# Gathers of a graph network issued in pairs, each pair behind a point of VectorE's work

## The chip, the cores and the metric

One core of a Trainium2 chip runs the whole program, in one launch. The metric is the device time of the launch in microseconds, the median of several runs; lower is better.

## What is computed

A graph of 3125 nodes and 100000 edges, sorted by destination. `x` (3125 x 64) goes through a graph transformer of four layers (hidden width 128, 8 heads of 16), is added to the input and normed, then goes through one message-passing layer, and is again added and normed. Cut to what matters here:

```python
h = gelu(x @ Wi.T + bi)
for i in range(4):                                   # the four layers
    q = (h @ Wq[i].T + bq[i])[dst]                   # per edge, 8 heads x 16
    k = (h @ Wk[i].T + bk[i])[src]                   # gathered per edge
    v = (h @ Wv[i].T + bv[i])[src]                   # gathered per edge
    alpha = sum(q * k, -1) / 4
    a = softmax of alpha over the edges with one dst
    out = segment_sum(a * v, dst)
    x_r = h @ Ws[i].T + bs[i]
    beta = sigmoid([out, x_r, out - x_r] @ Wbeta[i].T)
    h = layer_norm(beta * x_r + (1 - beta) * out + h)
    h = gelu(h @ W1[i].T + b1[i]) @ W2[i].T + b2[i] + h
x = layernorm(x + h @ Wo.T + bo)
msg = silu([x[src], x[dst], rbf(length)] @ mw1 + mb1) @ mw2 + mb2
agg = segment_sum(msg, dst) / count
out = layer_norm(silu([x, agg] @ uw1 + ub1) @ uw2 + ub2)
x = layernorm(x + out)
```

## The kernel before

**Places and chunks.** Nodes are held in 25 blocks of 128 (NB). The edges are cut into 806 places (PLACES) of 128 edges, so that the edges that a place counts have their destinations in one block. 16 places (CH) are a chunk; a pass over all edges has 51 chunks (CHUNKS), the last with 6 places. There are five passes: one for each of the four transformer layers and one for the messages. A chunk's places are handled in four groups of four (G, NG).

**The gather.** For each place GpSimd issues one indirect DMA (L508), which fetches 128 rows of a table in HBM into `slots`, one row a partition: 264 floats of keys and values from `kv_table` in a layer, 128 floats from `src_table` in the message pass. `slots` is a ring of four chunks (RING): chunk c lies in ring position c mod 4. The row numbers of a chunk (`idx`) are loaded by SyncE into the same ring.

**What a layer does with a chunk.** The functions called `attend_step` stand once for each engine, in the same order of chunks. While the step of chunk g is at work, chunk g + 1 is prepared:

- TensorE spreads the queries to the edges with turned one-hots (`spread_terms` L797, `rows` L806); VectorE multiplies them with the fetched keys (`multiply`, L1282, semaphore `spread_used`; it waits for the landing of the group's fetches, `kv_in`, and for the spread queries, `q_spread`) and sums over each head (`sum_heads`, L1288).
- VectorE scans for the running maxima, ScalarE takes exponentials; VectorE weighs the fetched values by them (`weigh`, L1361, `w_done`).
- TensorE multiplies the weighed values of each place with its one-hots (`add_up`, L825). The last matmul of a group frees the group's slots (`slot_free[k][j]`).
- VectorE adds the 16 products to `acc` (`add_place`, L1265, `acc_done` goes up by one a place).

In the message pass `messages` (L1416) takes the place of `multiply`, and there are no scans.

**A layer's head and end.** At the end of a layer VectorE, ScalarE and TensorE norm and feed forward in five groups of blocks. The next layer's keys and values are evicted to `kvst` (L1458) and stored by SyncE to `kv_table`; when all five stores have landed (`tab_out`) the next layer's fetches may go. `begin_layer` on VectorE then evicts the 25 blocks of queries (L1464, `q_ev` goes up by one a block), clears `acc` (L1467, `acc_zero`), makes the first one-hots, weighs 25 blocks (L1476), and multiplies the four groups of chunk 0. `acc` holds the activations that TensorE reads for the queries until then.

**What orders the fetches.** GpSimd's program holds nothing but the fetches until the end (`gather_chunk`). Fetches of a group of a chunk wait for the table, for the chunk's `idx`, and for `slot_free` of the same group four chunks before. So GpSimd may be up to four chunks ahead of VectorE's additions, and goes in fours:

```python
for j in range(groups):
    pool.wait_ge(slot_free[k][j], START + used[j])
    pool.reg_add(uses[k][j], uses[k][j], 1)
    for t in range(j * G, min((j + 1) * G, places)):
        pool.indirect_dma_start(slots[:, k, t, 0:width], None, table, ...)
```

All counted semaphores start at START, so that a wait for something before the first chunk is met at once.

Of the kernel before, what the change touches and what calls it, by code (L numbers as in the profile page):

```python
# [25 lines left out]
L = 4  # L26
HEADS, DH = 8, 16
HID = HEADS * DH
NB = -(-N // P)
# [3 lines left out]
CH = 16  # L33
RING = 4
CHUNKS = -(-PLACES // CH)
V = CHUNKS * CH
VC = -(-V // P)
FULL, REM = CHUNKS // RING, CHUNKS % RING
G = 4
NG = CH // G  # L40
# [13 lines left out]
ROUNDS = 4  # L54
LAST_PLACES = PLACES - (CHUNKS - 1) * CH
LAST_NG = -(-LAST_PLACES // G)
START = (RING - 1) * NG + 1
NBASIS = 16
STACK = P // NBASIS
HIDDEN = (4, 4, 6, 4, 6)  # L60
# [16 lines left out]
def build_program(nc, a, out):  # L77
    with ExitStack() as ctx:
# [3 lines left out]
        def sem(name):  # L82
            return ctx.enter_context(nc.semaphore(name))
# [166 lines left out]
        in_ps, in_act, s_ps, q_ev, h_ev = sem("in_ps"), sem("in_act"), sem("s_ps"), sem("q_ev"), sem("h_ev")  # L250
# [15 lines left out]
        node_done, acc_zero = sem("node_done"), sem("acc_zero")  # L266
# [5 lines left out]
        spread_used, alpha_done, alpha_turned = sem("spread_used"), sem("alpha_done"), sem("alpha_turned")  # L272
# [6 lines left out]
        ex_done, ex_turned, w_done = sem("ex_done"), sem("ex_turned"), sem("w_done")  # L279
        acc_scaled, acc_done, part_ps = sem("acc_scaled"), sem("acc_done"), sem("part_ps")  # L280
# [61 lines left out]
        def _(sp):  # L342
# [14 lines left out]
            def stage_indices(k, l, i):  # L357

                c = RING * i + k
                sp.wait_ge(spread_used, START + NG * (l * CHUNKS + c - RING + 1))  # L360
                load_indices(k, c)
# [20 lines left out]
            def load_layer(l):  # L382
                sp.wait_ge(h_new, START + 2 * NI * l)
                sp.dma_start(vec0[:, :], a["vec0"][bass.ds(l, 1), :].to_broadcast([P, VEC0_W])).then_inc(ld_layer, 16)
# [4 lines left out]
            def store_table(l):  # L389
                for i in range(NI):  # L390
                    sp.wait_ge(a_ev, START + NB * l + BW * (i + 1))
                    sp.dma_start(kv_table[i * GW:(i + 1) * GW, :].rearrange("(b p) k -> p b k", p=P),
                                 kvst[:, i * BW:(i + 1) * BW, :]).then_inc(tab_out, 16)

            def stage_first(l):
                sp.wait_ge(spread_used, START + NG * CHUNKS * l)
                for k in range(RING):
# [44 lines left out]
            with sp.Fori(0, L - 1) as l:  # L442
                stage_layer(l)
                stage_first(l + 1)
                sp.wait_ge(a_ev, START + NB * (l + 1))
                load_keys(l + 1)
                sp.wait_ge(q_ev, START + NB * (l + 1))
                load_queries(l + 1)
# [29 lines left out]
        def _(pool):  # L478
# [9 lines left out]
            for k in range(RING):  # L488
                for j in range(NG):
                    pool.reg_mov(uses[k][j], 0)  # L490

            def gather_chunk(k, turn, l, table, width, places=CH):
                groups = -(-places // G)
                used = [pool.snap(uses[k][j]) for j in range(groups)]
                if k == 2:
                    pool.wait_ge(su_termsd, 48)
                if k == 3:
                    pool.wait_ge(su_rstd, 16 * 2 * HEADS)
                pool.wait_ge(tab_out, 16 * NI * (l + 1))
                pool.wait_ge(idx_in[k], 16 * (turn + 1))  # L500
                for j in range(groups):
                    if isinstance(turn, int):
                        pool.wait_ge(slot_free[k][j], START + turn)
                    else:
                        pool.wait_ge(slot_free[k][j], START + used[j])
                        pool.reg_add(uses[k][j], uses[k][j], 1)
                    for t in range(j * G, min((j + 1) * G, places)):
                        pool.indirect_dma_start(slots[:, k, t, 0:width], None, table,  # L508
                                                bass.IndirectOffsetOnAxis(ap=idx[:, k, t:t + 1], axis=0))\
                            .then_inc(kv_in[k][j], 16)  # L510
# [1299 lines left out]
```

## Time and profile before

| | |
|---|---|
| time, median of 3 runs | 5630.9 us (5628.94 to 5631.05) |
| the profiled execution: span, first to last instruction | 7840.1 us |
| its own time | not listed beside the span; the span is 39% above the median |
| VectorE busy in it | 4037.4 us (51%) |
| TensorE busy in it (matmul) | 4625.7 us (59%) |
| GpSimd busy in it | 3849.3 us (49%) |
| fetches (indirect DMAs) | 4030 in five passes of 806 |
| granted TensorE clock, mean | 0.679 |

The profiled execution took much longer than the runs that were timed. Durations of single instructions can be read from it; how long the engines waited for each other in a timed run cannot be read from it directly. "Busy" leaves out the time in which an engine waits, and the idle time before an instruction is shown in brackets behind its row, with what ended it. The name "remote" stands for an end that the profile could not place.

### The profile page before, as it was taken

The numbers are of one execution on the slowest core, as the hardware profiler recorded it, in microseconds if no ns is written. First come the engines' busy times: TensorE is split into PE (matmuls) and PEld (weight loads), VectorE is DVE, ScalarE is ACT, GpSimd is POOL, SyncE is SP. The second block draws the span as 40 slices with busy tenths as digits, with TensorE's granted clock in tenths as the row PEclk, the third lists the DMA queues.
The fourth block names the chain that finished last, engine by engine and source line by source line (L and its number), as shares of the span: only waits on it lengthen the run. The fifth ranks groups of instructions, "written<-read, shape, count | busy, mean of one in ns | idle before, by whom it ended". The sixth has DMA issues, their size and how long they took to land.

```text
span 7840.1 us, 106032 instructions
## 1 busy us (share of the span) xinstructions
PE 4625.7 (59%) x22831; PEld 3727.9 (48%) x22832; DVE 4037.4 (51%) x11107; ACT 2769.9 (35%) x6493; POOL 3849.3 (49%) x4066
## 2 busy tenths in 40 slices
PE   4555555655556556555555565555555656666667
PEld 2444444534444445344444453444444545555555
DVE  4555555645555556455555565555555553333334
ACT  1333333423333334233333342333333432323333
POOL 3555555335555553345555543455555425555553
PEclk6666666676666666766666667666666677877887
DMA  5222222222322222222223222222322211111111
GB/s 127 78 79 76 77 76 78 52 66 73 79 78 77 78 80 56 69 67 79 76 78 79 78 62 69 68 78 77 80 78 79 60 33 43 44 44 44 44 44 30
DMA packets 267188, 536.13 MB, mean 68 GB/s; under 512 B 116253, under 2 KB 148689, under 8 KB 266509
## 3 DMA queue, kind: packets, MB, share of 16 engines
q0 software_dynamic: 180992, 490.24, 23.6%
q1 hardware_dynamic: 78901, 35.89, 1.9%
q10 hardware_dynamic: 6936, 6.69, 0.3%
q14 instruction: 314, 2.57, 0.1%
q8 instruction: 45, 0.74, 0.0%
HBM read 512.41 MB, written 18.03 MB: 68 GB/s over the span
## 4 chain that ended last, share of the span: by engine, by line
PE 26%; another core or an unknown queue 26%; issue 20%; DVE 17%; ACT 5%; DVEq 4%; ACTq 1%; SPq 0%; DMA 0%; POOL 0%; POOLq 0%
PE bank L806 9%; PE bank L825 7%; DVE acc L1265 6%; ACT oh L556 2%; DVEq L333 2%; PE bank L797 2%; PE bank L851 2%; PE bank L810 1%; DVE alpha L1288 1%; PE bank L879 1%; DVEq L1265 1%; DVE slots L1361 1%; DVE oh L1249 1%; PE bank L1001 1%
## 5 line engine op out<-in xcount | busy, mean ns | idle before, releaser
L508 POOL DMA_INDIRECT slots<-kv_table,idx x3224 | 3065.2, 951 | 3133.0 <-PE bank L825 1275.8
L825 PE MATMUL bank<-slots,oh 128*128 128x136 f32 (+1 forms) x8060 | 1593.0, 351 | 569.1 <-DVE acc L1265 506.4
L806 PE MATMUL bank<-qs,ohT 128*128 x8080 | 1685.7, 356 | 235.1 <-ACT ohT L547 129.2
L825 PEld LDWEIGHTS bank<-slots,oh 128*128 128x128 f32 x8060 | 1411.7, 252 | 704.7 <-DVE acc L1265 608.2
L806 PEld LDWEIGHTS bank<-qs,ohT 128*128 128x128 f32 x8080 | 1434.4, 257 | 456.6 <-issue 434.4
L1265 DVE TENSOR_TENSOR acc<-acc,bank 128x136 f32 (+1 forms) x4030 | 1172.0, 291 | 614.6 <-PE bank L825 171.5
L1282 DVE TENSOR_TENSOR slots<-slots,bank 128x512 f32<-128x512 f32 x808 | 551.8, 683 | 1322.6 <-remote 1291.5
L547 ACT ACTIVATE ohT<-bank,miss 128x512 f32<-128x512 f32 x1010 | 676.7, 683 | 1367.9 <-PE bank L797 1234.5
L508 POOL DMA_INDIRECT slots<-src_table,idx x806 | 760.4, 943 | 756.9 <-DMA idx<-src_e 247.9
L843 PE MATMUL bank<-ident,alpha 128*128 128x128 f32 x204 | 93.7, 459 | 1487.2 <-DVE alpha L1288 1481.7
L556 ACT ACTIVATE oh<-iota,rel_e 128x128 f32<-128x128 f32 x3168 | 962.8, 387 | 0.0
L843 PEld LDWEIGHTS bank<-ident,alpha 128*128 128x128 f32 x204 | 36.4, 178 | 1527.5 <-DVE alpha L1288 1521.6
L569 ACT COPY f_in<-bank 1x256 f32<-1x256 f32 x204 | 73.6, 361 | 1464.0 <-PE bank L851 723.1
L1361 DVE TENSOR_TENSOR slots<-slots,bank 128x544 f32<-128x544 f32 x808 | 575.9, 713 | 5.0
L1288 DVE TENSOR_REDUCE alpha<-slots 128x32 f32<-128x512 f32 x808 | 549.1, 680 | 0.6
L797 PE MATMUL bank<-terms,spread 12*128 12x512 bf16 x1010 | 519.8, 524 | 40.2 <-issue 32.8
L1416 DVE TENSOR_TENSOR slots<-slots,bank 128x512 f32<-128x512 f32 x202 | 138.4, 685 | 769.6 <-remote 426.3
L628 ACT ACTIVATE slots<-slots 128x512 f32<-128x512 f32 x202 | 127.1, 630 | 962.5 <-DVE slots L1416 915.4
L560 ACT ACTIVATE oh<-oh 128x1024 f32<-128x1024 f32 x396 | 418.4, 1057 | 12.8
L810 PE MATMUL bank<-resets 128*128 128x128 f32 x1616 | 403.5, 339 | 11.5 <-issue 11.3
L810 PEld LDWEIGHTS bank<-resets 128*128 128x128 f32 x1616 | 333.5, 254 | 9.6 <-issue 9.3
L879 PE MATMUL bank<-ident,ex 128*128 128x128 f32 x204 | 96.8, 474 | 257.9 <-ACT ex L586 249.2
(257 smaller groups left out, 4079.5 us busy)
## 6 DMA issues: line engine op xcount, KB each, us to landing
slots<-kv_table,idx POOLq DMA_INDIRECT x3224
kv_table<-slots SPq DMA_DIRECT2D x20, 660.0 KB, 3.4
slots<-src_table,idx POOLq DMA_INDIRECT x806
resets<-flat_len ACTq DMA_DIRECT2D x51, 128.0 KB
idx<-src_e SPq DMA_DIRECT2D x255, 8.0 KB
terms<-flat_rel SPq DMA_DIRECT2D x255, 12.0 KB
resets<-flat_rst SPq DMA_DIRECT2D x2, 1551.0 KB
w<-in_w SPq DMA_DIRECT2D x8, 256.0 KB
```

The lines of the kernel that those rows point to most:

```text
L508: pool.indirect_dma_start(slots[:, k, t, 0:width], None, table, bass.IndirectOffsetOnAxis(ap=idx[:, k, t:t + 1], axis=0))\
L547: act.activation(ohT[:, j % 2, :, :].rearrange("p a b -> p (a b)"), bank[j % 2][:, :], ACT.Relu, bias=miss[:, 0:1], scale=-1.0).then_inc(o ...
L556: act.activation(oh[:, k % 2, t, :], iota[:, :], ACT.Abs, bias=rel_e[:, bass.ds((prior + 1) * CH + t, 1)], scale=-1.0).then_inc(oh_far, 1 ...
L560: act.activation(tiles, tiles, ACT.Relu, bias=1.0, scale=-1.0).then_inc(oh_made, 1 + skipped)
L797: pe.matmul(bank[j % 2][:, :], spread[:, j, :], terms[:, k, :], start=True, stop=True)\
L806: mm = pe.matmul(o, ohT[:, j % 2, t, :], qs[:, blocks[j * G + t], 0:HID], start=True, stop=basis is None)
L810: mm = pe.matmul(o, rbf[:, k % 2, half, :], m_1c[:, q, :], start=False, stop=True)
L825: mm = pe.matmul(bank[6 + part % 2][:, o:o + width], oh[:, k % 2, t, :], slots[:, k, t, HID:HID + width], start=True, stop=True)
L1265: dve.tensor_tensor(a_t, a_t, bank[6 + part % 2][:, o:o + width], ALU.add)\
L1282: dve.tensor_tensor(keys, keys, bank[2 + j % 2][:, :].rearrange("p (t k) -> p t k", t=G), ALU.mult).then_inc(spread_used, counts_for(j, gr ...
L1288: dve.tensor_reduce(alpha[:, :, j * G:(j + 1) * G].rearrange("p h t -> p t h"), slots[:, k, j * G:(j + 1) * G, 0:HID].rearrange("p t (h d) ...
L1361: dve.tensor_tensor(vals, vals, bcl(exs[:, j * G:(j + 1) * G, :], VW), ALU.mult).then_inc(w_done, counts_for(j, groups))
```

## The change

GpSimd's fetches of a chunk go out as eight pairs. Ahead of each pair stands a further wait, on a count that VectorE drives. With g the number of the chunk that is fetched, over all passes, a layer's pair waits for:

| pair | the further wait |
|---|---|
| 0 | all additions of chunk g - 4 (`acc_done`) |
| 1 | the product of the first group of chunk g - 2, which is made in the step of chunk g - 3 (`spread_used`) |
| 2 | the second weighing of chunk g - 3 (`w_done`) |
| 3, 4, 5, 6, 7 | 2, 4, 6, 9, 12 additions of chunk g - 3 (`acc_done`) |

In ring position 0, pair p > 0 also waits for 3p of the layer's 25 query evictions (`q_ev`), in ring position 1 pair 0 waits for all 25, and pair 2 for the clearing of `acc` (`acc_zero`). They count at a layer's head alone: later in the layer they are met at once. In the message pass pair p waits for 2p additions of chunk g - 3. The waits for `slot_free` stay. The compared counts are kept in three registers.

```diff
-START = (RING - 1) * NG + 1
+START = (RING - 1) * CH + 1
+ADDS = (0, 0, 0, 2, 4, 6, 9, 12, CH)
...
+            next_add, next_product, next_weighing = [pool.alloc_register(n) for n in ("next_add", "next_product", "next_weighing")]
+            pool.reg_mov(next_add, START - CH * (RING - 1))
+            pool.reg_mov(next_product, START - NG * (RING - 2) + 1)
+            pool.reg_mov(next_weighing, START - NG * (RING - 1) + 2)
+
+            def keep_pace(l, k, pair, last):
+
+                product, weighing, added = pool.snap(next_product), pool.snap(next_weighing), pool.snap(next_add)
+                if k == 0 and pair > 0:
+                    pool.wait_ge(q_ev, START + NB * l + 3 * pair)
+                elif k == 1 and pair == 0:
+                    pool.wait_ge(q_ev, START + NB * (l + 1))
+                elif k == 1 and pair == 2:
+                    pool.wait_ge(acc_zero, START + l + 1)
+                if pair == 1:
+                    pool.wait_ge(spread_used, product)
+                    pool.reg_add(next_product, next_product, NG)
+                elif pair == 2:
+                    pool.wait_ge(w_done, weighing)
+                    pool.reg_add(next_weighing, next_weighing, NG)
+                else:
+                    pool.wait_ge(acc_done, added)
+                    pool.reg_add(next_add, next_add, (CH if last else ADDS[max(pair + 1, 3)]) - ADDS[pair])
+
+            def keep_last_pace(turn, k, pair):
+
+                if isinstance(turn, int):
+                    pool.wait_ge(acc_done, START + CH * (L * CHUNKS + FULL * RING + k - RING + 1) + 2 * pair)
+                    return
+                added = pool.snap(next_add)
+                pool.wait_ge(acc_done, added)
+                pool.reg_add(next_add, next_add, 2)
...
                     for t in range(j * G, min((j + 1) * G, places)):
+                        if t % 2 == 0:
+                            if isinstance(l, int):
+                                keep_last_pace(turn, k, t // 2)
+                            else:
+                                keep_pace(l, k, t // 2, places < CH)
                         pool.indirect_dma_start(slots[:, k, t, 0:width], None, table,
                                                 bass.IndirectOffsetOnAxis(ap=idx[:, k, t:t + 1], axis=0))\
```

GpSimd's program, in a layer, ring position 2 (any chunk but those at the head), before. A row of DMA stands for so many fetches; REGISTER_ALU and ISA rows are the sequencer's own.

```order
L505 REGISTER_ALU [waits idx_in2,tab_out,su_termsd]
L506 REGISTER_ALU [waits slot_free2_0]
L508 DMA slots<-kv_table,idx 128x264 x4
L505 REGISTER_ALU
L506 REGISTER_ALU [waits slot_free2_1]
L508 DMA slots<-kv_table,idx 128x264 x4
L505 REGISTER_ALU
L506 REGISTER_ALU [waits slot_free2_2]
L508 DMA slots<-kv_table,idx 128x264 x4
```

The same place in the changed program (the change adds 39 lines above this one):

```order
L539 REGISTER_ALU [waits idx_in2,tab_out,su_termsd]
L540 REGISTER_ALU [waits slot_free2_0]
L515 REGISTER_ALU [waits acc_done]
L547 DMA slots<-kv_table,idx 128x264 x2
L509 REGISTER_ALU [waits spread_used]
L547 DMA slots<-kv_table,idx 128x264 x2
L539 REGISTER_ALU
L540 REGISTER_ALU [waits slot_free2_1]
L512 REGISTER_ALU [waits w_done]
L547 DMA slots<-kv_table,idx 128x264 x2
L515 REGISTER_ALU [waits acc_done]
L547 DMA slots<-kv_table,idx 128x264 x2
```

Each four became two pairs, with one register instruction and one wait ahead of each pair. At ring position 0, where the fetches of a layer's head begin, the changed program reads:

```order
L534 ISA [waits tab_out]
L539 REGISTER_ALU [waits idx_in0]
L540 REGISTER_ALU [waits slot_free0_0]
L515 REGISTER_ALU [waits acc_done]
L547 DMA slots<-kv_table,idx 128x264 x2
L502 ISA
L509 REGISTER_ALU [waits spread_used,q_ev]
L547 DMA slots<-kv_table,idx 128x264 x2
L539 REGISTER_ALU
L540 REGISTER_ALU [waits slot_free0_1]
L502 REGISTER_ALU
L512 REGISTER_ALU [waits w_done,q_ev]
```

From the second pair on, each pair stands behind `q_ev` as well, with one more sequencer instruction; before, nothing stood between the table's landing and the fetches of the head.

## Rows read from the trace of the kernel before

**Rows 1.** The page: the span

```profile
span 7840.1 us, 106032 instructions
```

**Rows 2.** Waits, whole span: engine, line waited for, us in total, times, longest

```profile
DVE slots L1282 <- remote: 1291.5, 177, 8.1
...
POOL slots L508 <- issue: 1060.9, 3390, 1.2
```

**Rows 3.** Timeline, GpSimd: last fetch of a group, first of the next two

```profile
2598.41 0.95 POOL L508 DMA_INDIRECT slots<-kv_table,idx  x1 [0.30 <-issue]
2599.67 0.94 POOL L508 DMA_INDIRECT slots<-kv_table,idx  x1 [0.30 <-issue]
...
2607.01 0.94 POOL L508 DMA_INDIRECT slots<-kv_table,idx  x1 [2.65 <-remote]
```

**Rows 4.** Timeline, the same stretch: TensorE's spread queries, VectorE's product of them

```profile
2596.90 1.05 PE L806 MATMUL bank<-qs,ohT 128*128 x8
...
2606.16 0.69 DVE L1282 TENSOR_TENSOR slots<-slots,bank 128x512 f32<-128x512 f32 x1 [7.43 <-remote]
```

**Rows 5.** Timeline, VectorE: first product of two neighbouring chunks, fetches under way

```profile
771.86 0.68 DVE L1282 TENSOR_TENSOR slots<-slots,bank 128x512 f32<-128x512 f32 x1
...
799.00 0.68 DVE L1282 TENSOR_TENSOR slots<-slots,bank 128x512 f32<-128x512 f32 x1
```

**Rows 6.** VectorE, fetches done: products of chunk 49 (groups 0, 3), 50 (groups 0, 1)

```profile
1525.55 0.69 DVE L1282 TENSOR_TENSOR slots<-slots,bank 128x512 f32<-128x512 f32 x1
...
1534.24 0.68 DVE L1282 TENSOR_TENSOR slots<-slots,bank 128x512 f32<-128x512 f32 x1
...
1544.21 0.68 DVE L1282 TENSOR_TENSOR slots<-slots,bank 128x512 f32<-128x512 f32 x1
...
1546.87 0.69 DVE L1282 TENSOR_TENSOR slots<-slots,bank 128x512 f32<-128x512 f32 x1
```

**Rows 7.** VectorE, messages, fetches done: chunks 48 and 49 (group 0), 49 (group 3)

```profile
7760.64 0.69 DVE L1416 TENSOR_TENSOR slots<-slots,bank 128x512 f32<-128x512 f32 x1 [3.33 <-PE bank L810]
...
7777.54 0.69 DVE L1416 TENSOR_TENSOR slots<-slots,bank 128x512 f32<-128x512 f32 x1 [3.45 <-PE bank L810]
...
7786.17 0.69 DVE L1416 TENSOR_TENSOR slots<-slots,bank 128x512 f32<-128x512 f32 x1 [0.50 <-PE bank L810]
```

**Rows 8.** Timeline, GpSimd: first fetches of layers 0 and 1, of the messages; fetches 21, 65

```profile
53.34 1.63 POOL L508 DMA_INDIRECT slots<-kv_table,idx  x1 [23.79 <-DMA idx<-src_e]
...
80.62 0.95 POOL L508 DMA_INDIRECT slots<-kv_table,idx  x1 [0.30 <-issue]
...
185.23 0.94 POOL L508 DMA_INDIRECT slots<-kv_table,idx  x1 [49.91 <-PE bank L825]
...
1651.74 0.94 POOL L508 DMA_INDIRECT slots<-kv_table,idx  x1 [157.38 <-DMA kv_table<-slots]
...
6396.38 0.94 POOL L508 DMA_INDIRECT slots<-src_table,idx  x1 [168.71 <-DMA src_table<-slots]
```

**Rows 9.** Timeline, VectorE, head of layer 0: queries, clearing, first product

```profile
73.39 0.74 DVE L1464 TENSOR_TENSOR qs<-bank,vec_qs 128x256 f32<-128x256 f32 x2
...
78.32 0.42 DVE L1464 TENSOR_TENSOR qs<-bank,vec_qs 128x256 f32<-128x256 f32 x1 [0.64 <-issue]
...
151.31 0.97 DVE L1464 TENSOR_TENSOR qs<-bank,vec_qs 128x256 f32<-128x256 f32 x2 [0.24 <-PE bank L966]
...
153.08 2.89 DVE L1467 MEMSET acc<- 128x3400 f32 x1 [0.66 <-issue]
...
164.53 0.69 DVE L1282 TENSOR_TENSOR slots<-slots,bank 128x512 f32<-128x512 f32 x1
```

**Rows 10.** Timeline, VectorE, head of layer 1: queries 1 and 11 of 25

```profile
1650.04 0.42 DVE L1464 TENSOR_TENSOR qs<-bank,vec_qs 128x256 f32<-128x256 f32 x1 [3.62 <-PE bank L966]
...
1658.91 0.42 DVE L1464 TENSOR_TENSOR qs<-bank,vec_qs 128x256 f32<-128x256 f32 x1 [1.01 <-PE bank L966]
```

**Rows 11.** GpSimd's register instructions of L505: times, ns min/median/max

```profile
L505 POOLq ALU_OP  x1000: 32/32/51, 52.5 to 7671.1; - x167
```

## The prediction

> **What bounds the kernel now.** I began with the span against the timed runs, since here they disagree: the profiled execution spans 7840.1 us [rows 1], the median is 5630.9 us, 2209 us less. So the trace holds waits that the timed runs do not have, and the first task is to find which. The list of waits names the largest one of VectorE that has no known cause: 1291.5 us in 177 pieces ahead of the product L1282, "remote" [rows 2]. The timelines of one such piece show it from both sides. TensorE began the last spread queries (L806) at 2596.90 and had 1.05 us of work, but VectorE's product of them started at 2606.16, after 7.43 us of idling [rows 4]. In those microseconds GpSimd was issuing fetches, and its next group started 0.85 us after VectorE's product [rows 3]. The same shows at a layer's head: query evictions came 1.07 us apart up to 78.32, and then the 25 took until 151.31 [rows 9], while the 64 fetches that began at 53.34 went out back to back. So, while fetches run in the profiled execution, the results of TensorE's work reach the others late.
>
> I take two rates from places where this does not happen. Behind a layer's last fetch a step takes 1544.21 - 1525.55 = 18.7 us [rows 6], against 27.1 us with fetches under way [rows 5]. A message step takes 7777.54 - 7760.64 = 16.9 us [rows 7]. The third rate is GpSimd's own: one fetch starts 1.25 us after the other (2599.67 - 2598.41, inside a run of neighbours and over a group's border alike) [rows 3], 0.3 us of it the gap that the waits list 3390 times [rows 2]. That is **20.0 us for a chunk of 16**, slower than either step.
>
> Sum on the assumption that GpSimd is the bound and TensorE is not held up. A pass is 806 x 1.25 = 1007.5 us of fetches; the fourth group of the last full chunk is there after 1000. From its product to the last product VectorE needs 1546.87 - 1534.24 = 12.6 us [rows 6], and from there to the next pass's first fetch the trace has 1651.74 - 1546.87 = 104.9 us [rows 6, 8]. Four layers: 4 x 1117.5 = 4470. Before them 53.3 us [rows 8], behind them 1000 us of messages and 7840.1 - 7786.17 = 53.9 us of end [rows 1, 7]. Together **5577 us, 54 us (1.0%) under the median**. Were GpSimd free, 50 steps of a layer would take 935 us and some 30 of head instead of 1000, and the messages 845 and some 40: about 5320, 310 us under the median. So I read the timed runs as bound by GpSimd's issue of fetches in every pass. The working below is in this unprofiled frame; the profiled span cannot be compared with it.
>
> **The change, part by part.**
>
> *Waits in the steady state: nothing.* While GpSimd is the bound, VectorE waits, in the step of chunk x - 1, for the fetches of chunk x that GpSimd is issuing. The new waits ask for points of the step of x - 3 at most, two steps ago. The same holds in the message pass.
>
> *Waits at the head of layers 1 to 3: about 1 us each.* The first fetch starts at 1651.74 [rows 8], the queries at 1650.04; the first ten gaps average (1658.91 - 1650.04) / 10 = 0.89 us [rows 10], so three queries take 2.7 us against 2.5 for a pair. The 25th is done at 1650.04 + 24 x 0.89 + 0.42 = 1671.8. Fetch 17, which now waits for it, would have started at 1651.74 + 20 = 1671.7; with the 0.85 us of a restart [rows 3, 4] it is 1 us late. Clearing `acc` ends 153.08 + 2.89 - 151.31 - 0.97 = 3.7 us behind the last query [rows 9], within the 5 us until fetch 21. The first product comes 164.53 - 152.28 = 12.3 us behind the last query [rows 9], at 1684, and fetch 35, which asks for it, at 1695. Fetch 51 at 1715 asks for a point of the next step, which begins before 1684 + 18.7. Nothing else stops it. Bounds: 0, and 5 us each if the queries come at 1.07 us [rows 9] (25th at 1676.1, fetch 17 at 1677.0).
>
> *Waits at the head of layer 0: 24 us.* Here GpSimd was early: it starts at 53.34, and fetch 21 at 80.62 [rows 8], but the queries start at 73.39 [rows 9]. Now only two fetches go before them. The sixth query ends at 78.7, the 25th 19 x 1.07 later, at 99.1; fetch 17 starts at 100, fetch 21 at 105, and `acc` is cleared at 102.8. That is **24 us later than 80.62**. It does not come back: layer 0 was bound by fetches at its end (fourth group of the last full chunk at 53 + 1000 = 1053; VectorE alone would be there at about 111 + 25 + 48 x 18.7 = 1034), and now more so. Bounds: 18 us, if the queries come at the 0.42 us that VectorE needs for one; 24 at the pace of rows 9, which I take since it was read at this very place. Fetches 1 (1.63 instead of 0.95 us [rows 8]) and a few more were lengthened by VectorE's casts beside them; up to 2 us of this may be saved, which I leave in the range.
>
> *Instructions added: nothing, covered by the fetches.* A chunk away from the head gets eight waits and eight register instructions more, about one each per pair; ring position 0 gets seven more. Such an instruction takes 32 ns [rows 11]. Two of them stand before each group already, and the group that starts at 2599.67 follows with the same 0.30 us gap as a fetch within a group [rows 3]: the sequencer does them while fetches are carried out. A pair has 2.5 us. If that cover failed, 11 x 32 ns a chunk, 255 chunks, would be 90 us.
>
 The rows here do not show the depth.
>
> *The late results of TensorE.* In the trace, splitting fetches so that gaps fall between them should release TensorE's results sooner, and the profiled span should shrink. In the timed runs I give nothing for it: by the sum above the hold-up is not there, or is hidden behind the fetches. Most that it could hide is the 54 us that the sum leaves open.
>
> The Trainium skill (SBUF — State Buffer, section "SBUF: two separate sides") says that engine ports and DMA ports are disjoint and cannot contend. By that rule the data of the fetches could not hold up TensorE at all and pacing them gains nothing, which is the 5658 below. The trace's 7.43 us do not fit the rule, but they are absent from the time.
>
> Sum: 5630.9 + 24 + 3 = **5658 us** (+0.5%); from the bounds 5649 to 5670. A difference under 0.2%, 11 us, could not be told from none.
>
> **The rivals.**
>
> *Faster: the hold-up is real and GpSimd is quicker than its rows.* The 0.30 us gap may be the recorder's, not the chip's. If a fetch took 0.95 us, a chunk would be 15 us, GpSimd would be far ahead in the timed runs too, and the 310 us above the free sum would be TensorE held up by bursts of fetches. Paced pairs could give back half or more: 5631 - 155 = 5476, at most 5321. For it: the trace shows such a hold-up 177 times and more, and the pairs go just where it hurts. Against: the sum with 1.25 us meets the median within 1% with nothing fitted. It decides if GpSimd's issue is under 18.7 us a chunk. Chance 0.15.
>
> *No change.* A step in the timed runs takes a little over 20 us for some other reason, and GpSimd has slack. Then the 24 us are lost while nobody waits: first product at 111, chunk 0 there at 100. 5631, within 11. Chance 0.18.
>
> *Slower by more: the sequencer's work shows.* Each pair's wait and registers delay the next fetch, since a fetch that stands behind a wait can't be prepared. With the 90 us above: 5658 + 90 = 5748; more if waits themselves cost. For it: in the timed runs GpSimd has no slack to hide it in. Against: rows 3. It decides from about 30 ns a pair. Chance 0.16.
>
> *The change does not do what it says* (a register off by a chunk, so that waits are always met) would give 5631; 0.02. My forecast: 0.49.
>
> **How the numbers follow.** Slower: 0.49 + 0.16 = 0.65. Within 0.2%: 0.18 + 0.02 = 0.20. Faster: 0.15. The range goes from 5600 (half of the 54 us gained, over half of the faster case left out) to 5760 (the upper rival with its 90 us).
>
> **What the changed profile would show.** Right: in layer 0, fetch 3 not before 75, fetch 21 near 105; in later layers no second run of 64 fetches; in the span, shorter idling before L1282, and queries closer together, so a span well under 7840 us beside a time that is not shorter. GpSimd's gap between fetches of different pairs 0.30 us where no wait holds it. Wrong: gaps over 0.35 us between pairs whose waits are long met (the upper rival); a time under 5600, which would mean that fetches were not the bound.

## The result and the profile after

| | before | changed |
|---|---|---|
| median of 6 runs | 5630.8 us | 5648.2 us |
| lowest to highest | 5628.1 to 5632.4 | 5646.3 to 5651.3 |
| profiled execution: span | 7840.1 [rows 1] | 5649.4 |

Changed over before is 1.0031, 95% interval 1.0020 to 1.0043: 17.4 us slower. The forecast was 5658, 27 us slower.

First the page of the changed kernel: the span, the chain that ended last by engine and by line, and the groups of fetches and products (all lines of the code stand 39 further down than before: L508 is now L547, L1282 is L1321, L1464 is L1503).

```profile
span 5649.4 us, 110477 instructions
...
PE 22%; issue 21%; POOL 21%; DVE 18%; DMA 6%; DVEq 5%; ACT 4%; POOLq 1%; ACTq 1%; SPq 0%
...
L547 POOL DMA_INDIRECT slots<-kv_table,idx x3224 | 3069.2, 952 | 1366.4 <-issue 1237.2
...
L1321 DVE TENSOR_TENSOR slots<-slots,bank 128x512 f32<-128x512 f32 x808 | 552.4, 684 | 95.9 <-DMA slots<-kv_table,idx 90.5
```

The product L1321 used to wait 1291.5 us for "remote" [rows 2]. That group is gone. What is left ahead of it is 90.5 us, and its releaser is the transfer that GpSimd issues: VectorE waits for fetches, as the sum of the prediction had it for the timed runs. The chain line does not say as much (only 21% of it is POOL, GpSimd's fetches); experiment 4 shows why that line misleads here. The profiled execution took 5651.3 us, 1.9 more than its span, so this trace shows what a timed run does, which the one of before did not.

The head of layer 0, on GpSimd's timeline of the changed kernel (start, duration, line, idling before it and its releaser). It answers to [rows 8]:

```profile
53.66 1.48 POOL L547 DMA_INDIRECT slots<-kv_table,idx  x1 [23.97 <-issue]
55.44 0.95 POOL L547 DMA_INDIRECT slots<-kv_table,idx  x1 [0.30 <-issue]
75.13 0.95 POOL L547 DMA_INDIRECT slots<-kv_table,idx  x1 [18.74 <-DVE qs L1503]
...
98.39 0.95 POOL L547 DMA_INDIRECT slots<-kv_table,idx  x1 [0.30 <-issue]
...
153.57 0.95 POOL L547 DMA_INDIRECT slots<-kv_table,idx  x1 [0.31 <-DVE acc L1304]
```

GpSimd idles for 18.74 us before fetch 3, until VectorE has evicted three queries. Fetch 21 starts at 98.39 where it was 80.62 [rows 8]; I had put it at 105. The queries themselves, on VectorE's timeline, answer to [rows 9] ("x2" is two instructions in one row):

```profile
72.20 0.75 DVE L1503 TENSOR_TENSOR qs<-bank,vec_qs 128x256 f32<-128x256 f32 x2
73.93 0.42 DVE L1503 TENSOR_TENSOR qs<-bank,vec_qs 128x256 f32<-128x256 f32 x1 [0.98 <-PE bank L1005]
...
77.13 0.42 DVE L1503 TENSOR_TENSOR qs<-bank,vec_qs 128x256 f32<-128x256 f32 x1 [0.64 <-PE bank L1005]
77.80 0.97 DVE L1503 TENSOR_TENSOR qs<-bank,vec_qs 128x256 f32<-128x256 f32 x2 [0.24 <-PE bank L1005]
79.02 0.98 DVE L1503 TENSOR_TENSOR qs<-bank,vec_qs 128x256 f32<-128x256 f32 x2 [0.24 <-issue]
...
88.75 0.42 DVE L1503 TENSOR_TENSOR qs<-bank,vec_qs 128x256 f32<-128x256 f32 x1 [0.24 <-PE bank L1005]
```

They come 1.07 us apart only up to 77.13. From 77.80 on two take 79.02 - 77.80 = 1.22 us, so 0.61 each, and the 25th is done at 89.2, not at 99.1. Three queries then take 1.8 us, less than the 2.5 us of a pair of fetches, so after the stop at fetch 3 the queries hardly hold anything up again: fetch 21 comes 18 fetches, 22.5 us, and 0.8 us more behind fetch 3.

### The profile page after: what moved, and what is told of

Its sections match the earlier page's. It is cut to its first block, busy times and chain, and to the rows that moved or that the text cites. A ratio compares the mean times of both kernels' runs of the same rounds, so it can differ in the third digit from the quotient of the medians.

```text
span 5649.4 us, 110477 instructions
## 1 busy us (share of the span) xinstructions
PE 4326.6 (77%) x22831; PEld 3528.5 (62%) x22832; DVE 4032.6 (71%) x11107; ACT 2774.7 (49%) x6493; POOL 3856.3 (68%) x4066
## 4 chain that ended last, share of the span: by engine, by line
PE 22%; issue 21%; POOL 21%; DVE 18%; DMA 6%; DVEq 5%; ACT 4%; POOLq 1%; ACTq 1%; SPq 0%
POOL slots L547 21%; PE bank L845 7%; DVE acc L1304 7%; PE bank L864 5%; DMA slots<-kv_table,idx 4%; DVEq L334 3%; DMA slots<-src_table,idx 2%; ACT oh L595 2%; PE bank L890 2%; PE bank L1040 1%; PE bank L918 1%; DVEq L1304 1%; DVE fb_out L1354 1%; DVE fwd L1377 1%; DVE bwd L1379 1%
## 5 line engine op out<-in xcount | busy, mean ns | idle before, releaser
L547 POOL DMA_INDIRECT slots<-kv_table,idx x3224 | 3069.2, 952 | 1366.4 <-issue 1237.2
L864 PE MATMUL bank<-slots,oh 128*128 128x136 f32 (+1 forms) x8060 | 1514.1, 337 | 321.1 <-DVE acc L1304 318.7
L845 PE MATMUL bank<-qs,ohT 128*128 x8080 | 1639.6, 349 | 106.0 <-ACT ohT L586 36.1
L864 PEld LDWEIGHTS bank<-slots,oh 128*128 128x128 f32 x8060 | 1333.4, 239 | 439.6 <-DVE acc L1304 399.5
L845 PEld LDWEIGHTS bank<-qs,ohT 128*128 128x128 f32 x8080 | 1391.3, 251 | 305.2 <-issue 283.2
L547 POOL DMA_INDIRECT slots<-src_table,idx x806 | 763.4, 947 | 371.1 <-issue 341.8
L1321 DVE TENSOR_TENSOR slots<-slots,bank 128x512 f32<-128x512 f32 x808 | 552.4, 684 | 95.9 <-DMA slots<-kv_table,idx 90.5
L1400 DVE TENSOR_TENSOR slots<-slots,bank 128x544 f32<-128x544 f32 x808 | 577.3, 715 | 10.5
L836 PE MATMUL bank<-terms,spread 12*128 12x512 bf16 x1010 | 485.5, 489 | 72.2 <-issue 63.4
L849 PE MATMUL bank<-resets 128*128 128x128 f32 x1616 | 363.7, 312 | 0.0
L849 PEld LDWEIGHTS bank<-resets 128*128 128x128 f32 x1616 | 297.9, 230 | 0.0
L1377 DVE TENSOR_TENSOR_SCAN fwd<-resets,icol,bank 128x128 f32<-128x128 f32 (+1 forms) x204 | 97.9, 480 | 247.4 <-issue 241.8
L890 PE MATMUL bank<-ident,fwd 128*1 128x128 f32 x204 | 63.8, 313 | 244.2 <-DVE bwd L1339 208.2
L918 PEld LDWEIGHTS bank<-ident,ex 128*128 128x128 f32 x204 | 37.2, 182 | 338.9 <-ACT ex L625 338.9
```

The source lines that it names most:

```text
L836: pe.matmul(bank[j % 2][:, :], spread[:, j, :], terms[:, k, :], start=True, stop=True)\
L845: mm = pe.matmul(o, ohT[:, j % 2, t, :], qs[:, blocks[j * G + t], 0:HID], start=True, stop=basis is None)
L849: mm = pe.matmul(o, rbf[:, k % 2, half, :], m_1c[:, q, :], start=False, stop=True)
L864: mm = pe.matmul(bank[6 + part % 2][:, o:o + width], oh[:, k % 2, t, :], slots[:, k, t, HID:HID + width], start=True, stop=True)
L1321: dve.tensor_tensor(keys, keys, bank[2 + j % 2][:, :].rearrange("p (t k) -> p t k", t=G), ALU.mult).then_inc(spread_used, counts_for(j, gr ...
L1400: dve.tensor_tensor(vals, vals, bcl(exs[:, j * G:(j + 1) * G, :], VW), ALU.mult).then_inc(w_done, counts_for(j, groups))
```

## The experiments

My theory: a pass is as long as its fetches (1.25 us each), the waits in the steady state are met long before, and the 17 us are lost once, in the head of layer 0. Its rivals: the waits and registers of all pairs cost a little each; TensorE is held up by bursts of fetches and pairs would help; the bound is not GpSimd. All experiments ran beside fresh runs of the kernel before, which took 5618 to 5619 us there (5630.8 beside the changed kernel), so differences are given against those. The edits are in GpSimd's loop unless said otherwise.

**1. The kernel before, once more.** No edit.

> The kernel before, unchanged. Time: 5631, within 0.1% by every theory. The question is its profiled span, 7840.1 us in the first profile against 5649.4 for the changed kernel. If the late results of TensorE come with recording this order of fetches, the span is about 7800 again; if that one recording was an accident, it is about 5630 and the trace of before must be read with that in mind.

Measured: 5618.7 beside 5619.0 us (ratio 1.0000, 0.9991 to 1.0009), and a profiled span of 5616.2 us. The page of this second recording:

```profile
span 5616.2 us, 106032 instructions
...
POOL 63%; issue 24%; PE 5%; DVE 4%; POOLq 2%; DMA 2%; ACT 1%; SPq 0%; DVEq 0%; ACTq 0%
POOL slots L508 63%; PE bank L1001 1%; PE bank L958 1%; PE bank L990 1%; DMA resets<-flat_rst 1%; POOLq L505 1%; POOLq L506 0%; DVE acc L1265 0%; DVE slots L1512 0%; POOLq L494 0%; DVE slots L1518 0%; POOLq L500 0%; DVE slots L1516 0%; DVE slots L1458 0%; PE bank L825 0%
```

So the 7840.1 us of [rows 1] and TensorE's late results of [rows 4] belonged to that one recording. The same program recorded again does not have them. What caused them is open. In this trace the bound can be read off: 63% of the chain is the fetch L508, and "issue" is mostly the 0.30 us between fetches.

It is also the right trace to hold against the changed one. GpSimd at the head of layer 0, fetches 21 and 65, in the trace of before taken again:

```profile
80.33 0.95 POOL L508 DMA_INDIRECT slots<-kv_table,idx  x1 [0.30 <-issue]
...
134.14 0.95 POOL L508 DMA_INDIRECT slots<-kv_table,idx  x1 [0.30 <-issue]
136.77 0.94 POOL L508 DMA_INDIRECT slots<-kv_table,idx  x1 [1.68 <-DMA idx<-src_e]
```

Fetch 65 is at 136.77 here and at 153.57 in the changed kernel: 16.8 us, practically the whole difference of 17.4. At fetch 21 it is 18.1 us; the kernel before then loses 1.4 us at fetch 65, where it idles for 1.68 us until the indices of chunk 4 are there, and the changed kernel, being later, does not. Behind fetch 65 the two traces part further, to 33.2 us in the span. They come from different sets of runs, and the kernel before alone differs by 12.1 us between these (5630.8 and 5618.7), so nothing is read from that; the trace of experiment 3 is the one to compare in full. From the start of fetch 1 to the end of the last, layers 0 to 3 take 1012.3, 1009.8, 1010.3 and 1011.7 us here, the messages 1007.1, and 806 x 1.25 is 1007.5.

**2 and 3. Without the head's waits, and with these alone.** Experiment 2 takes these lines out of the changed kernel. Experiment 3 keeps them and takes out all other added waits and `keep_last_pace` (beside each head wait stand one register instruction and one wait that is long met).

```diff
-                if k == 0 and pair > 0:
-                    pool.wait_ge(q_ev, START + NB * l + 3 * pair)
-                elif k == 1 and pair == 0:
-                    pool.wait_ge(q_ev, START + NB * (l + 1))
-                elif k == 1 and pair == 2:
-                    pool.wait_ge(acc_zero, START + l + 1)
```

> The changed kernel without the three waits at a layer's head (for queries and for the clearing of acc); the other waits stay. My theory (the 17 us are lost in layer 0's head, where fetches that used to be early now wait for queries): fetch 21 starts at about 81 us again, only fetch 35 still waits, for the first product at about 102 instead of 96, so 6 us stay: about 5637. Rival (the 17 us come from the waits and register instructions of all pairs, spread over the passes): about 5648, as with all waits.

> Only the waits at a layer's head; of the other pairs nothing is waited for (one register instruction stays beside each head wait). My theory: the loss is all there, 16 to 19 us, so about 5648. Rival (spread over the pairs): 5631 to 5634.

Measured: without them 5624.0 us, 5.0 over before (ratio 1.0010, 1.0001 to 1.0019). With them alone 5636.5, 17.5 over (1.0033, 1.0021 to 1.0045). So the head's waits are the whole loss. The trace of experiment 3, from the same set of runs as that of before taken again, has it at the head too:

```profile
151.58 0.95 POOL L528 DMA_INDIRECT slots<-kv_table,idx  x1 [0.30 <-issue]
```

That is fetch 65, 99.2 us behind fetch 1 where it is 83.3 us in the kernel before: 15.9 us, of 17.7 in the span (5633.9 against 5616.2). The 5.0 us of experiment 2 show in one place of the trace of experiment 2, GpSimd's timeline at fetches 34 and 35:

```profile
96.70 0.94 POOL L541 DMA_INDIRECT slots<-kv_table,idx  x1 [0.30 <-issue]
104.10 0.94 POOL L541 DMA_INDIRECT slots<-kv_table,idx  x1 [6.46 <-DVE slots L1315]
```

The first product (L1315 there) starts at 102.65 and takes 0.69 us, and the fetch that asks for it starts 0.76 us after its end, 6.15 us later than without the wait (96.70 + 1.25); 1.4 us of that come back at fetch 65. Behind the head's waits this one costs nothing, since fetch 35 then comes at 115.9 anyway: the two losses lie beside each other and do not add.

**4. As many waits, all long met.** Every register advances by 1 instead of by what the chunk adds, and the head's waits ask for the count of the layer's start.

```diff
-                    pool.wait_ge(q_ev, START + NB * (l + 1))
+                    pool.wait_ge(q_ev, START + l)
...
-                    pool.reg_add(next_product, next_product, NG)
+                    pool.reg_add(next_product, next_product, 1)
...
```

> The changed kernel with the same number of waits and register instructions, but every added wait asks for a value reached long before (registers advance by 1). My theory (the sequencer does them while a fetch is carried out, nothing is held): 5631, within 3 us. Rival (the instructions themselves cost): 5640 or more, up to 5720 at 32 ns each. Its profiled span tells more: if holding fetches back is what freed TensorE in the recording, it is about 7800 us; if the added instructions between fetches did, about 5630.

Measured: 5618.8 beside 5619.0 us (1.0000, 0.9991 to 1.0009), span 5616.5. The added instructions cost nothing. The recording has no hold-up either, which says nothing any more, since experiment 1 shows none for the kernel before. Its page shows something else:

```profile
PE 23%; issue 21%; POOL 20%; DVE 20%; DVEq 5%; DMA 5%; ACT 4%; POOLq 1%; ACTq 0%; SPq 0%
```

This is nearly the chain line of the changed kernel, for a kernel whose added waits were all met long before and whose time is that of before. In its list of waits 431 fetches stand behind the usual gap of 0.30 us and yet are put down to an addition of VectorE, though none of them had to wait for one; in the changed kernel it is 418. From such a fetch the chain goes on to VectorE and TensorE. So the chain of 63% POOL in the kernel before and that of 21% in the changed one are no sign of different bounds.

Whether the waits of the changed kernel are met early can be counted in its trace, from the end of the awaited instruction to the start of the pair's first fetch. The waits for queries and for the clearing of `acc` aside, the shortest such time in layers 0 to 3 is 10.7 us (layer 0, chunk 3), in the messages 34.3 us, and the middle of a layer has 24 to 32 us.

**5 and 6. Part of the fetches taken from GpSimd.** In the kernel before, SyncE copies the rows of places 12 to 15 (in experiment 5 of ring position 3 alone, in experiment 6 of all; the edit is that of 6, the copies of a pass's first four chunks and the condition for the last chunk are left out here).

```diff
+                sp.wait_ge(slot_free[k][NG - 1], START + turn_of(l, i, k, NG - 1))
+                for t in range(CH - COPIED, CH):
+                    sp.dma_start(slots[:, k, t, 0:width], table[0:P, :]).then_inc(kv_in[k][NG - 1], 16)
...
-                    for t in range(j * G, min((j + 1) * G, places)):
+                    for t in range(j * G, min((j + 1) * G, places, CH - COPIED)):
```

> The kernel before, but places 12 to 15 of every chunk of ring position 3 are not fetched by GpSimd: SyncE copies rows 0 to 127 of the table there, the same bytes from wrong rows. That leaves the right rows of those places out. GpSimd issues 48 fetches fewer in a pass, 18.75 us a chunk instead of 20. My theory (its issue bounds every pass): attention passes become bound by the 18.7 us step, about 42 us less each, the message pass 60 us less: about 5390 beside 5619 of before on this chip. Rival (a step takes 20 us for another reason): 5619, no change.

> The same for all four ring positions, so that GpSimd issues 12 fetches of a full chunk, 15 us. My theory: steps of 18.7 and 16.9 us bound the passes, about 310 us less than before, 5310; nothing more is to be had by fetching faster. If it comes out under 5250 the steps are quicker than the 18.7 us that I read; over 5450, something that grows with the data and not with GpSimd's issue is in the way. Rival (another reason): 5619.

Measured: 5456.0 us for ring position 3 (0.9700, 0.9683 to 0.9717), 5381.6 for all (0.9577, 0.9561 to 0.9593). The same bytes move, GpSimd issues less, and the time falls by 163 and 237 us: GpSimd's issue was the bound. The copies are plain and read neighbouring rows, so the two runs alone do not part GpSimd's issue from the way in which the rows are fetched. Experiment 10 comes from the other side: there only GpSimd's instructions change. Both fell less than I had expected (5390 and 5310). A free attention step is 19.15 us on average, not 18.7, since a few steps take 24 to 26 us (from the first weighing of each chunk in the trace of experiment 6, the last chunk of a layer left out); a message step is 17.1 instead of 16.9. And in experiment 6 the first copies came late: the first product of layer 0 waited 25.0 us for one. In VectorE's waits of experiment 6:

```profile
DVE slots L1299 <- DMA slots<-kv_table: 25.0, 1, 25.0
```

The page of experiment 6 has the chain of a kernel that fetches do not bound:

```profile
PE 35%; DVE 27%; issue 18%; DVEq 9%; ACT 8%; ACTq 1%; DMA 1%; POOL 0%; SPq 0%; POOLq 0%
```

The Trainium skill (Perfetto Trace Analysis, DMA Optimizations) advises that where descriptor generation is the bottleneck, spreading DMAs over several issuing engines may help. The runs agree as far as they go, with 237 us for plain copies issued by SyncE. It is no version to keep, because these copies take wrong rows: SyncE's copies here know nothing of `idx`.

**7. The changed kernel with the same copies.** The edit of 6 on the changed kernel.

> The changed kernel with the same copies. Here GpSimd has slack, so that it could run ahead and the pairs' waits decide when it fetches. If bursts of fetches held TensorE up (the rival of my prediction), it is faster than the kernel with the copies alone, by 50 us or more. My theory: no hold-up, the pacing waits are met in time: the same within 10 us, since even the loss in layer 0's head is made up by a GpSimd that is faster than the steps. A third way: each wait held late costs when GpSimd would be ahead, 20 us or more slower.

Measured: 5373.0 us (0.9563, 0.9547 to 0.9579), 8.6 under experiment 6, with intervals that overlap. GpSimd now does stand at a pair's wait, 840.2 us at pair 1's, for the first product of a chunk: its list of waits has

```profile
POOL slots L564 <- DVE slots L1338: 840.2, 192, 25.0
```

and in experiment 6, without pairs, it stood about as long for freed slots:

```profile
POOL slots L525 <- PE bank L842: 848.7, 302, 33.4
```

So the pairs move the place where GpSimd waits. That costs nothing, because GpSimd has the time, and it gains nothing that can be told. If bursts of fetches held TensorE up, I had put the gain at 50 us and more.

**8 and 10. More waits ahead of every fetch.** In the kernel before, 8 of them, and 24 in experiment 10 (`counted` is the list of semaphores that start at START).

```diff
+                        for s in counted[:8]:
+                            pool.wait_ge(s, 1)
                         pool.indirect_dma_start(slots[:, k, t, 0:width], None, table,
```

> The kernel before with eight more waits ahead of every fetch, each on another semaphore and long met. At about 32 ns for each of some seven further instructions that is 0.22 us of GpSimd's sequencer per fetch. My theory (done while the fetch before is carried out): 5619, within 3 us. Rival (they add to the fetch): 7 x 32 ns x 4030 = 900 us more, about 6520.

> The kernel before with 24 waits ahead of every fetch, on 24 semaphores, all long met: some 23 instructions more for a fetch, at 32 ns 0.74 us. With 8 waits nothing showed. My theory: 0.74 us still lies within the 1.25 us of a fetch, 5619, within 5 us. Rival (the sequencer's cover is less than that, for instance the 0.30 us between fetches and some more): each 0.1 us uncovered costs 403 us, so 6000 or more.

Measured: with 8 waits 5618.1 beside 5618.6 us (1.0009, 0.9991 to 1.0028), nothing; one of its ten runs took 5666.5, the others 5614.5 to 5624.9. With 24 waits 7080.3 us (1.2604, 1.2583 to 1.2625): 1462 us more. I had expected nothing here too, and that failed. Two waits share an instruction, so it is 12 for a fetch, as their row in experiment 10 counts (48364 / 4030 = 12.0; ns min/median/max):

```profile
L509 POOLq EVENT_SEMAPHORE  x48364: 17/43/43, 52.3 to 7029.6; - x200
```

and GpSimd's timeline of experiment 10 has fetches 1.47 to 1.78 us apart instead of 1.25 (1.62 on average within a pass, with the longest steps where a group or a chunk begins):

```profile
1500.61 0.94 POOL L510 DMA_INDIRECT slots<-kv_table,idx  x1 [0.66 <-issue]
1502.08 0.95 POOL L510 DMA_INDIRECT slots<-kv_table,idx  x1 [0.53 <-issue]
1503.55 0.95 POOL L510 DMA_INDIRECT slots<-kv_table,idx  x1 [0.52 <-issue]
1505.33 0.94 POOL L510 DMA_INDIRECT slots<-kv_table,idx  x1 [0.84 <-issue]
```

while in experiment 8, with 4 such instructions, nothing has moved:

```profile
1500.88 0.95 POOL L510 DMA_INDIRECT slots<-kv_table,idx  x1 [0.30 <-issue]
1502.13 0.94 POOL L510 DMA_INDIRECT slots<-kv_table,idx  x1 [0.30 <-issue]
```

The sequencer works beside the fetches until its own work for one is over 1.25 us. Twelve at 43 ns are only 0.52 us, but the starts of these instructions in the trace of experiment 10 show where the rest is. They start 87 ns apart (at 1500.467, 1500.553, 1500.640 and so on to 1501.333), twice the length of their records, and from the start of the last one to that of the next fetch's first, at 1501.877, it is 0.54 us. From the first at 1500.406 that makes 0.93 + 0.54 = 1.47 us, the step of the fetches. So 4 fit and 12 do not; by these steps about 9 would (0.54 + 8 x 0.087 = 1.24 us), an estimate that no run tested.

**9. The head's delay made larger.** In the changed kernel the pairs of ring position 0 all wait for the 25th query.

```diff
-                    pool.wait_ge(q_ev, START + NB * l + 3 * pair)
+                    pool.wait_ge(q_ev, START + NB * (l + 1))
```

> The changed kernel, but the pairs of ring position 0 all wait for the layer's 25th query instead of for 3, 6, 9 and so on, so that only two fetches go before the queries are done. In the profile of before, repeated, the 25th query of layer 0 is done at 91.2 us and fetch 3 started at 56.6; in layer 1 it is done at 1195.3 and fetch 3 started at 1182.0. With 0.8 us of a restart, my theory (a pass is as long as its fetches, and a fetch that starts late stays late) gives 35 us in layer 0 and 14 us in each of layers 1 to 3: 77 us over before, about 5696 beside 5619. Rival (VectorE's steps have enough slack to take in a head's delay in layers 1 to 3, and only layer 0 counts): 5654.

Measured: 5690.6 us beside 5618.4 (1.0128, 1.0111 to 1.0145), 72.2 more where 77 were expected. GpSimd's timeline has the stops of fetch 3 in layers 0 and 1:

```profile
88.69 0.95 POOL L547 DMA_INDIRECT slots<-kv_table,idx  x1 [33.07 <-DVE qs L1503]
...
1229.11 0.94 POOL L547 DMA_INDIRECT slots<-kv_table,idx  x1 [13.84 <-DVE qs L1503]
```

From fetch 1 to fetch 65 it takes 34.0, 14.1, 14.8 and 10.5 us over 80 in layers 0 to 3. In the trace of before taken again that is 3.3 and then 0.1 to 0.2, so the heads lose 69.7 us, and the time 72.2. A late start in any layer is paid in full.

**11. More work on VectorE.** In the kernel before, `sum_heads` of group 1 gets a second reduction into a tile of its own.

```diff
+                if j == 1:
+                    for m in range(1):
+                        dve.wait_ge(spare_done, START + 1 * g + m)
+                        dve.tensor_reduce(spare_sum[:, m, :], slots[:, k, j * G:(j + 1) * G, 0:HID], axis=X, op=ALU.add).then_inc(spare_done, 1)
```

> The kernel before with one more reduction on VectorE in every attention step, 0.68 us, 204 times, its result unused. A free step took 19.15 us on average in the kernel with all copies, so it becomes 19.83, just under the 20.0 us of GpSimd's fetches. My theory: hidden in layers 1 to 3 (up to 3 us each), while in layer 0, where VectorE begins late, 120.7 + 50 x 19.83 = 1112 against 1096 costs 16 us: 5635 to 5645. Rival (VectorE or the chain through it bounds the steps): 204 x 0.68 = 139 us more, 5758.

Measured: 5630.2 us beside 5618.4 (1.0021, 1.0012 to 1.0031), 11.7 more of the 139 that were added; I had expected 16 to 26. The place is the expected one: layer 0's last fetch starts at 1064.6 us as before (1064.7), but the first weighing of its last chunk is 12 us later (1107.7 against 1096.0), and the fetches of layer 1 begin at 1190.9 instead of 1179.5. Of the 34 us added to the 50 steps of layer 0 (50 x 0.68) 12 show: VectorE's steps begin late there and have little slack against the fetches. The later layers take the added work in.

**12. An earlier first fetch.** In the kernel before, VectorE's setup:

```diff
-            for i in range(NI):
+            for i in range(NI - 1):
                 projected_keys(0, i)
+            dve.wait_ge(su_rows, 16 * VC)
+            dve.tensor_copy(r_src, rows_i).then_inc(su_turn, 1)
+            projected_keys(0, NI - 1)
+            for k in range(VC):
+                take(k)
             dve.wait_ge(su_blk, 1)
...
-            dve.wait_ge(su_rows, 16 * VC)
-            dve.tensor_copy(r_src, rows_i).then_inc(su_turn, 1)
...
-            for k in range(VC):
-                take(k)
```

> A version meant to be quicker: the kernel before, with the setup's source rows cast ahead of the last group of key evictions and turned right behind them, ahead of the casts of blocks and destinations, so that the indices land sooner and GpSimd's first fetch starts at about 50 instead of 53.4 us. My theory (every us by which a pass's fetches start earlier is a us off the time, as every late one was a us on it): layer 0's last fetch 3.5 us earlier, 5615 beside 5619, which the comparison can just not tell from none, but the trace can. Rival (layer 0 is no longer bound by fetches when they start earlier): the last fetch of layer 0 earlier, the first fetch of layer 1 not.

Measured: 5618.1 beside 5618.0 us (1.0000, 0.9991 to 1.0009). The first fetch does start earlier, but fetch 65 does not. GpSimd's timeline of experiment 12:

```profile
50.12 1.18 POOL L508 DMA_INDIRECT slots<-kv_table,idx  x1 [20.40 <-DMA idx<-src_e]
...
130.79 0.95 POOL L508 DMA_INDIRECT slots<-kv_table,idx  x1 [0.30 <-issue]
137.83 0.94 POOL L508 DMA_INDIRECT slots<-kv_table,idx  x1 [6.09 <-DMA idx<-src_e]
```

Neither case that I had written down says this. The 3.3 us are given back at fetch 65, which opens the second turn of the ring and waits for the indices of chunk 4. SyncE issues their load late: in its program it stands behind a wait for the landing of the last setup loads, issued from 86.77 on (its timeline of experiment 12):

```profile
86.77 2.57 SPq L438 DMA_DIRECT2D resets<-flat_rst  x4
130.65 0.57 SPq L368 DMA_DIRECT2D idx<-src_e  x1
```

The load also asks for the four products of chunk 0, but these are done at 108.5. The kernel before had this stop too, 1.68 us [experiment 1]. Loading chunk 4's indices ahead of the wait for the setup loads might give some 4 us. That was not tried, and it is near what a comparison can tell. No version here with the right rows beats the kernel before. The large gain of experiments 5 to 7 needs fewer fetches on GpSimd.

## Why the prediction was right, and where not

- **The bound** (1.25 us a fetch, 20.0 us a chunk, passes of 1007.5 us): right. Experiments 5 and 6 show it by what falls when GpSimd issues less, experiment 10 by what grows with its instructions alone (4030 fetches start 0.36 us further apart and the time grows by all of it, 1462 us, so there was no slack against them), the trace of experiment 1 by its passes of 1007 to 1012 us. The sum left 54 us open. 39 of them stand in that trace. 24 lie between the passes: the next pass's first fetch starts 113.5 to 114.8 us after a pass's last, and 126.9 before the messages, where the sum had 111. 15 lie within the four layers, whose fetches come a little over 1.25 us apart. Another 12 are the difference between the two sets of runs of the kernel before, and the last 2.5 that between its span and its time.
- **The floor without GpSimd's bound** (5320): too low. Experiment 6 has 5381.6, some 25 of it from its own late copies. The step of 18.7 us had been read at one place.
- **Waits in the steady state: nothing.** Right: experiment 2 leaves 5.0 us, all at fetch 35, before the steady state, and the waits of the changed kernel are met at least 10.7 us early (experiment 4).
- **Heads of layers 1 to 3: about 1 us each.** Too high and of no weight. The first 64 fetches took 0.3, 0.6 and 0.5 us over 80 in the changed kernel. The queries come 0.61 us apart, so the 25th is done before fetch 17 is due.
- **Head of layer 0: 24 us.** The mechanism was right (fetch 3 not before 75 us: it starts at 75.13), the size was off: 17.8 us at fetch 21, 16.8 at fetch 65, 17.4 in the time. The term that failed is "the 25th 19 x 1.07 later". The pace was read at this place, but over the first few queries, since those after them were held up in the recording, and I carried it over to all. In the changed kernel it holds up to the sixth query and is 0.61 from there on. The lower bound, 18 us from VectorE's 0.42 us each, was the nearer end, and for a reason: as soon as three queries take less than a pair's 2.5 us, only the stop at fetch 3 is left, whatever their pace.
- **Instructions added: nothing, covered.** Right (experiments 4 and 8). The price behind it was not. The prediction counts 16 instructions more for a chunk and then prices 11; GpSimd's records are 4436 more than before, 17.4 a chunk, which at 32 ns would be 142 us and not 90. And a wait is 43 ns in its record and 87 ns from start to start, not the 32 ns of a register instruction [rows 11], so that 12 a fetch are too many (experiment 10).
- **TensorE's late results: absent from the time.** Right, but they were absent from the kernel altogether. "A span well under 7840" came true for a reason that is not the change's (experiment 1). My faster rival drew its 0.15 from those rows.
- **The rule of two SBUF sides.** The Trainium skill (SBUF — State Buffer, section "SBUF: two separate sides") says that the ports of engines and DMA cannot contend. The prediction held the 7.43 us of [rows 4] against it; they did not come back, and experiment 7 finds no gain in pacing. So no run here speaks against the rule any more; none tests it on its own.
- **The queue of 8** (Trainium skill, Advanced Engine Details and Errata, Engine Queue Depths). I drew from it that a wait met a little late costs nothing. That is not borne out: the one late wait of experiment 2 was late by 5.4 us and cost 5.0 us of the time. From the awaited product's end to the fetch it has 0.76 us against the usual gap of 0.30, so a late wait costs about 0.5 us besides its delay. No run here shows the depth of the queue.

## What to carry to other kernels

Before a trace is read for causes, compare its span with the timed runs; where they differ by more than a few us, record the kernel again before giving any wait in it a chance. Do not compare two chains where one kernel has more waits than the other: a kernel with waits that hold nothing (experiment 4) gets a different chain and the same time. Where one engine's issue bounds a pass, look at when its stream starts and who can stop it before it is in step: a wait there is paid once and in full, while waits on points two steps back were free here. A stream that starts earlier gains only if every later gate is open too, so follow it to its next wait first.

## What the runs showed of the hardware

- GpSimd's indirect DMA of 128 rows takes 0.95 us and repeats every 1.25 us, the same for 1056-byte rows (952 ns mean) and for 512-byte rows (947 ns).
- Semaphore waits ahead of it are free up to at least 4 instructions (8 waits) per fetch; with 12 (24 waits) the period grows to 1.25 + 1462 / 4030 = 1.61 us on average, and the kernel by 26%. Their records are 43 ns long and start 87 ns apart.
- A fetch behind a wait that is met late starts 0.76 us after the end of the VectorE instruction that it waits for (experiment 2).
- One recording of a kernel was 39% longer than its timed runs, with waits of up to 8.1 us ahead of one product [rows 2] that the next recording of the same kernel does not have.
